# A convolution block in front of an expert stage: tap logits after the convolution in one run, an exponential, transposes and a sum moved

## The reference

```
u  = (x - mean_c(x)) / sqrt(var_c(x) + 1e-6)            # over channels, per pixel
wt = softmax over an axis of length 1 of ((max(u) @ w2.T + b2) - (avg(u) @ w1.T + b1))
x  = x + depthwise_conv3x3(u, wt) + bias + u            # a 3x3 filter per image and channel
t  = tokens of x (32768 rows of 128)
n  = layernorm(t);  gates = n @ Wg + bg;  best two of 8 experts, softmax of their gates
out = t + sum over both of weight * (gelu(n @ W1[e] + b1[e]) @ W2[e] + b2[e])
```

## Time and profile before

| | |
|---|---|
| median of 3 runs | 1534.79 us (1530.91 to 1535.08) |
| the profiled execution | 1534.89 us, its span 1532.4 us |
| PE busy over the span | 1453.9 us (95%) |
| DVE busy | 1308.8 us (85%) |
| ACT busy | 1096.7 us (72%) |
| POOL busy | 961.6 us (63%) |

### The profile page before, as it was taken

One profiled execution on the slowest core, in us unless ns is written; L12 is line 12 of the kernel. 1 busy time (PEld: TensorE's weight loads), 2 busy tenths in 40 slices (PEclk: granted clock), 3 DMA queues, 4 the chain that ended last, 5 costly groups with the idle time before them and its releaser, 6 DMA issues.

```text
span 1532.4 us, 45755 instructions
## 1 busy us (share of the span) xinstructions
PE 1453.9 (95%) x12204; PEld 1114.6 (73%) x12205; DVE 1308.8 (85%) x2676; ACT 1096.7 (72%) x2514; POOL 961.6 (63%) x1069
## 2 busy tenths in 40 slices
PE   5999999999999867999999999999999999999996
PEld 2345454555545433999999999999999999999995
DVE  2468888888888984999999999999989999999995
ACT  5477777878777523777777777777777777777773
POOL 2004455545555674777777777777777777777773
PEclk8899999999999955999999999999999999999998
DMA  4211212121222127111111232223232322222222
GB/s 141 74 38 57 70 63 81 63 75 58 77 69 64 40 71 151 41 47 40 44 43 57 66 93 86 92 86 93 85 94 83 92 86 91 84 86 78 78 75 109
DMA packets 85647, 115.77 MB, mean 76 GB/s; under 512 B 17613, under 2 KB 69865, under 8 KB 85590
## 3 DMA queue, kind: packets, MB, share of 16 engines
q1 hardware_dynamic: 64886, 76.83, 17.0%
q0 software_dynamic: 18112, 34.27, 7.0%
q10 hardware_dynamic: 2592, 4.00, 0.9%
HBM read 60.08 MB, written 58.48 MB: 77 GB/s over the span
## 4 chain that ended last, share of the span: by engine, by line
POOL 38%; PE 24%; issue 23%; DVE 6%; ACT 4%; DMA 2%; POOLq 2%; SPq 1%; ACTq 0%; DVEq 0%
PE psV L902 14%; POOL token_out L542 14%; POOL xn L530 14%; POOL yt L537 9%; PE psA L840 4%; PE psV L849 3%; DVE x L1235 2%; POOL rows_by_pair L512 1%; ACT cv L628 1%; PE psT L884 1%; ACT diag L618 1%; PE psG L886 1%; DMA stage<-in_L_ffn_W_dram 1%; ACT lnv L601 1%; POOLq L542 1%
## 5 line engine op out<-in xcount | busy, mean ns | idle before, releaser
L1495 DVE TENSOR_TENSOR gl<-g,gh 128x512 f16<-128x512 f32 x620 | 489.1, 828 | 71.1 <-ACT gh L777 61.2
L512 POOL DMA_INDIRECT rows_by_pair<-rows,idx x256 | 263.6, 1030 | 318.7 <-issue 196.1
L542 POOL DMA_INDIRECT token_out<-yt,rt x310 | 338.7, 1093 | 184.7 <-POOL yt L537 133.6
L902 PE MATMUL psV<-lp,diag 128*128 128x512 f32 x576 | 274.4, 613 | 20.5 <-ACT cv L628 20.5
L777 ACT ACTIVATE gh<-g 128x512 f16<-128x512 f32 x465 | 274.5, 624 | 16.8
L770 ACT ACTIVATE g<-psT 128x512 f32<-128x512 f32 x310 | 182.2, 597 | 101.3 <-PE psT L1057 74.4
L770 ACT ACTIVATE g<-psV 128x512 f32<-128x512 f32 x310 | 184.8, 597 | 90.1 <-PE psV L1057 62.0
L530 POOL TENSOR_SCALAR xn<-rt 128x128 f32<-128x128 f32 x310 | 221.5, 721 | 14.0 <-DMA rt<-rows_by_pair 10.1
L1078 PE MATMUL psR<-wall,gh 128*128 x1240 | 221.3, 273 | 0.4 <-DVE ya L1512 0.4
L1078 PE MATMUL psG<-wall,gh 128*128 x1240 | 221.3, 273 | 0.0
L902 PEld LDWEIGHTS psV<-lp,diag 128*128 128x128 f32 x576 | 106.2, 193 | 150.9 <-issue 108.2
(11 more groups left out here) (231 smaller groups left out, 2950.2 us busy)
## 6 DMA issues: line engine op xcount, KB each, us to landing
rt<-rows_by_pair SPq DMA_DIRECT2D x155, 133.0 KB, 2.1
xb<-in_x_dram SPq DMA_DIRECT2D x32, 512.0 KB, 3.5
yq<-token_out SPq DMA_DIRECT2D x112, 128.0 KB, 2.4
out_dram<-oq SPq DMA_DIRECT2D x112, 128.0 KB
token_out<-yt,rt POOLq DMA_INDIRECT x310, 2.3
rows_by_pair<-rows,idx POOLq DMA_INDIRECT x256, 2.4
stage<-in_L_ffn_W_dram SPq DMA_DIRECT2D x1, 2048.0 KB, 8.3
ye<-token_out SPq DMA_DIRECT2D x4, 512.0 KB, 4.3
```

The costliest lines, as they stand in the source:

```text
L512: gp.indirect_dma_start(rows_dram, bass.IndirectOffsetOnAxis(ap=idx[p][:, b:b + 1].bitcast(U32), axis=0), rows[p][:, b, :], None).then_inc ...
L542: gp.indirect_dma_start(y_dram, bass.IndirectOffsetOnAxis(ap=rt[r][:, b, ID:ID + 1].bitcast(U32), axis=0), yt[r][:, b, :], None, bounds_ch ...
L902: ins = te.matmul(psConv.rearrange("p (h w) -> p h w", w=WW), diag[k][:, m, :], lp[j][:, y:y + HH // 2, dx:dx + WW], start=(m == 0), stop= ...
L1495: v.tensor_tensor(gl[side][q][:, cols], g[side][:, cols], gh[side][q][:, cols], ALU.subtract).then_inc(lo_done, 1)
```

## The change

Five edits of the order, with the same operations on the same data. On PE all taps of the second image come first, then all 36 tap-logit matmuls, then the centring; and for the first image (k = 0) six blocks of transposes instead of five stand ahead of the variance, the other two are moved between the convolution's halves, and two taps instead of one stand ahead of the second variance. On ACT the tap exponential moves from the end of the step to a place ahead of the second image's last copy, and the first image's `token_std` and `keep` move ahead of its `sum_up`. On DVE the product in `own_places` and the reduction in `number` are only marked, and the sum `den` of the two gate exponentials moves from `weigh` to `number`, ahead of `idx`.

```diff
+    TURN_0 = 6
...
@@ ACT, step
-                    if st_.on(1):
+                    if k == 1 and st_.on(1):
                         sum_up(st_, k)
                     if st_.on(3):
                         token_std(st_, k)
                         keep(st_, k)
+                    if k == 0 and st_.on(1):
+                        sum_up(st_, k)
+                    if k == 1 and st_.on(1):
+                        act.wait_ge(z_ready, st_.count(1, 1, 1))
+                        sc_.activation(ez[:, :, :], zd[:, :, :], ACT.Exp).then_inc(ez_ready, 1)
                     if st_.on(2):
                         take(st_, k, 1)
...
                 if st_.next().on(1):
                     square(st_.next(), 0)
-                if st_.on(1):
-
-                    act.wait_ge(z_ready, st_.count(1, 1, 1))
-                    sc_.activation(ez[:, :, :], zd[:, :, :], ACT.Exp).then_inc(ez_ready, 1)
@@ PE, step (tap_logits loses its quarters and runs all taps)
                     if st_.on(3):
-                        turn(st_, k, 0, TURN_1)
+                        turn(st_, k, 0, TURN_1 if k else TURN_0)
                     if st_.on(1):
                         variance(st_, k, 0)
-                    if st_.on(3):
+                    if k == 1 and st_.on(3):
                         turn(st_, k, TURN_1, NBLK)
...
                     if st_.on(2):
-                        conv(st_, k, 0, 0)
+                        for m in range(2):
+                            conv(st_, k, 0, m)
                     if k == 0 and st_.on(1):
                         variance(st_, k, 1)
...
-                        for m in range(1, len(taps_pe[k])):
+                        for m in range(2, len(taps_pe[k])):
                             conv(st_, k, 0, m)
+                    if k == 0 and st_.on(3):
+                        turn(st_, k, TURN_0, NBLK)
...
-                        for m in range(len(taps_pe[0]) if k == 0 else N_PE - 2):
+                        for m in range(len(taps_pe[k])):
                             conv(st_, k, 1, m)
...
-                for quarter in range(4):
-                    if quarter < 2:
-                        if st_.on(2):
-                            conv(st_, 1, 1, N_PE - 2 + quarter)
-                    elif st_.next().on(1):
-                        centre(st_.next(), 0, quarter - 2)
-                    if st_.on(1):
-                        tap_logits(st_, quarter)
+                if st_.on(1):
+                    tap_logits(st_)
+                if st_.next().on(1):
+                    for h in range(2):
+                        centre(st_.next(), 0, h)
@@ DVE, own_places and number (den leaves weigh)
-                c4.link(v.tensor_tensor(pos[:, :, :], pos[:, :, :], pairs[:, :, :], ALU.mult))
+                c4.mark(v.tensor_tensor(pos[:, :, :], pos[:, :, :], pairs[:, :, :], ALU.mult))
...
-                link(v.tensor_reduce(idf[:, :], pos[:, :, :], AX_X, ALU.add))
+                c4.wait()
+                c4.mark(v.tensor_reduce(idf[:, :], pos[:, :, :], AX_X, ALU.add))
+                dve.wait_ge(e2_ready, st_.count(4, 1, 1))
+                c4.link(v.tensor_tensor(den[:, :], e2[:, :, 0], e2[:, :, 1], ALU.add))
```

More of the change, by code:

```diff
@@ L856, in setup_done, with tap_logits @@
                 pe.wait_ge(s_setup_dve, 2)
[L858 to L865, removed]
+            def tap_logits(st_):
+                pe.wait_ge(pool16_ready, st_.count(1, 1, 1))
+                if st_.on(4):
+                    pe.wait_ge(rank_read, st_.count(4, 1, 1))
+                for tap in range(TAPS):
                     at = R_TAP + 4 * tap
@@ L870, in tap_logits @@
                         last = te.matmul(psR[:, at:at + 2], cwT[:, a, tap, 1, :], both[:, 0:2], start=False, stop=(a == 1), skip_group_check=True)
-                if quarter == 3:
-                    last.then_inc(tap_ready, 1)
+                last.then_inc(tap_ready, 1)
             def turn(st_, k, first=0, end=NBLK):
@@ L1301, in own_places @@
             def own_places(st_):
-                c4.link(v.tensor_tensor(pos[:, :, :], pos[:, :, :], pairs[:, :, :], ALU.mult))
+                c4.mark(v.tensor_tensor(pos[:, :, :], pos[:, :, :], pairs[:, :, :], ALU.mult))
             def number(st_):
-                link = c4.link
-                link(v.tensor_reduce(idf[:, :], pos[:, :, :], AX_X, ALU.add))
+                c4.wait()
+                c4.mark(v.tensor_reduce(idf[:, :], pos[:, :, :], AX_X, ALU.add))
+                dve.wait_ge(e2_ready, st_.count(4, 1, 1))
+                c4.link(v.tensor_tensor(den[:, :], e2[:, :, 0], e2[:, :, 1], ALU.add))
                 if not st_.fixed or (st_.turns(4) > 0 and not st_.last(4)):
@@ L1318, in weigh @@
                 r_ = rows[st_.row_slot(4)]
-                dve.wait_ge(e2_ready, st_.count(4, 1, 1))
-                link(v.tensor_tensor(den[:, :], e2[:, :, 0], e2[:, :, 1], ALU.add))
                 link(v.reciprocal(wa[:, :], den[:, :]))
```

## The result

The changed kernel takes 1511.98 us (median of 4 runs, 1510.42 to 1513.72) against 1533.7 (1530.91 to 1535.08): a ratio of 0.9861, 95% interval 0.9842 to 0.988. The chip's engines go by two names here: PE is TensorE, DVE is VectorE, ACT is ScalarE. The profiled execution took 1510.42 with a span of 1507.6, 24.8 less than the span of before.

A forecast was written before the change was run, and what follows sets the result against it. PE was taken to bound the step, 31.16 us. Gains of 0.12 and 0.85 make 0.97; times 14 is 13.6, less 0.3 plus 0.2 gives 13.5: 1534.9 to 1521.4 us, range 1516 to 1529.

The forecast's parts named there:

- The sum of the step: PE's step of 31.16 us less 0.12 for tap logits and 0.85 for transposes: 30.19, a gain of 0.97.
- I take nothing: ACT's exponential ahead of the last copy: 0 to 0.2 us to spare before PE's variance, counted as no gain or loss.
- the two places named: PE's losses per step: 0.94 us waiting for ACT's copy before the convolution's second half, 0.27 before the second variance.
- the rival on DVE: DVE sets the pace, so its whole 1.39 us wait leaves every step: 19.5 us, total 1515.4; chance 0.07.
- PE's pieces don't fit into 29.8: Argument against DVE setting the pace: PE's work needs about 30.2 us a step, DVE's chain without its wait 29.8.
- the 0.27 that was booked under the two taps: PE's wait before the second variance; two taps instead of one give ACT 0.88 us longer, removing it.
- The exponential's chain: ACT's exponential, copy, then square finished at t = 22.93 us; PE reaches the variance at 22.95, so it just fits.
- The late square: Rival: ACT's square delays PE's variance, each step giving back 0.3 us; gain 9.3, total 1525.6; chance 0.18.
- The slower rival: Exponential stays at t = 22.37 us and blocks ACT's copy and square; 0.4 more per step, total 1540.6; chance 0.07.
- First tokens: ACT's first-image tokens ahead of its sum: costs nothing; PE reaches the second image's transposes no sooner than the centring before.
- DVE's edits: DVE's idle 0.19 and 0.21 us go; 0 in the loop, 0.2 gained on the path to the scatter.
- Start and tail: 12 more tap logits ahead of the second centring half lose 0.3 us; DVE edits add 0.2 at the end.

The follow-up runs named there:

- the load runs: Changed kernel (period 29.77) plus two additions on VectorE each step: 29.77; plus three of the second image's transposes done twice on TensorE: 30.09.
- TURN_0 = 5: Changed kernel with three blocks of transposes behind the convolution instead of two, five ahead of the first variance: period 29.63, 1508.11 us, ratio 0.9845.

## Why the prediction was too small

Three steps of it failed. The sum of the step carried a stretch over as unchanged in which PE was waiting, and priced taps and variances too high. "I take nothing" for the exponential missed that it is a link of the round trip that set the pace. The clock at the start had no term. Of the 8.2 us by which the medians miss the forecast, the step makes 14 x 0.42 = 5.9.

*What bounds the kernel before.* PE does lose time at the two places named. That its own work sets the pace there does not hold: by the two runs with additions on DVE (0.00 and 0.39) it was the round trip over PE, DVE and ACT. In the changed kernel PE does set the pace, at 29.77, so the sentence against the rival on DVE, "PE's pieces don't fit into 29.8", was wrong. The rival's time for a step (1.39) came out and its mechanism did not: two additions on DVE, ahead of its wait, cost nothing in either kernel. That the gain of a step equals DVE's wait is luck. The rule beside it (the Trainium skill, Perfetto Trace Analysis, Identifying the Most-Contended Engine: judge TensorE by MFU and weight loads, not by matmul busy time) would, by the weight loads, have named DVE; the load runs do not agree with it in the changed kernel, +0.33 for TensorE against nothing for VectorE.

*The sum of the step:* 0.97 forecast, 1.39 measured. By stretches of PE's timeline, in one step each:

| stretch | before | forecast | after |
|---|---|---|---|
| convolution to convolution (267.94 / 283.52) | 14.93 | 14.93, unchanged | 14.73 |
| last convolution, logits, centring | 6.42 | 6.30 | 6.25 |
| transposes to the next convolution | 9.81 | 8.96 | 8.79 |

The missing 0.42 is 0.20 + 0.05 + 0.17. The last two are prices: a tap inside a run costs 0.86 (two taps from 307.12 to 308.84, three from 309.70 to 312.27), and the 0.88 had the start of a run behind a wait in it; the variance between the taps costs 0.86 (308.84 to 309.70), not 0.95. The 0.20 is work called unchanged in which PE was in fact waiting. The weight load ahead of the second image's transposes, before and after, and ACT's last operation on the first image's tokens:

```profile
274.06 0.14 PEld L884 LDWEIGHTS psT<-ident,x 128*128 128x128 f32 x1 [0.67 <-issue]
```

```profile
273.75 0.20 ACT L656 ACTIVATE rows<-rstd 128x8 f32<-128x8 f32 x1
```

```profile
289.21 0.14 PEld L883 LDWEIGHTS psT<-ident,x 128*128 128x128 f32 x1 [0.24 <-issue]
```

```profile
287.87 0.20 ACT L657 ACTIVATE rows<-rstd 128x8 f32<-128x8 f32 x1
```

The load is idle 0.43 less, under a name that tells of no wait. But `turn` waits for ACT to have kept the first image's tokens, and in the kernel before the load comes 0.11 to 0.12 behind the end of that operation in each of eight steps; in the changed kernel it comes 1.14 behind it. So it waited for the first tokens; in the run with the transposes alone the profile names this wait (PE psT <- ACT rows). As means of six and seven steps the stretch shrinks by 0.15 (14.92 to 14.76), between the centring and the convolution behind the transposes; in the two steps of the table a shorter wait for ACT's copy, 0.19 against 0.27, adds to it.

*By edits* the split was further off. Logits and exponential were to bring 0.12 and brought 0.72; the transposes were to bring 0.85 and brought 0.67 behind them, nothing without them. The prediction took the exponential only as a possible cost ("I take nothing"); it was the half of the round trip that freed diagonals, logarithm and second variance, and so also the 0.27 that was booked under the two taps: with these two edits and still one tap ahead of it, the second variance starts 0.95 behind that tap, not 1.19.

*The exponential's chain* held: exponential, copy and square in time, no wait before the variance, with 0.45 to spare where it "just fits". The late square came only with a third block moved. *The slower rival* is what the exponential does without the early logits: right in kind, 0.9 a step at full clock, far more with the clock's fall.

*First tokens* cost nothing, as said, and the changed kernel is as fast without that edit. The sentence that PE reaches the second image's transposes no sooner than the centring before them did not hold for the kernel before, as the weight load shows; with the exponential moved alone, first tokens as before, the load is idle 0.25 already.

*DVE's edits* bring nothing in the loop, as said, and the 0.2 at its end was right. From the last row of the pattern to the scatter it is 18.39 in three kernels that have them (the changed one twice, and with the first tokens as before) and 18.64 in the two that don't. By the Trainium skill's rule beside it (VectorE: DVE Perf Modes, The DRAIN you can't avoid) they bring nothing; the trace does not agree there. Whether the 0.25 reaches the end of the span the runs don't show: from the last exponential to there it is 1025.0 and 1024.7 us in the two runs of the changed kernel and 1024.7 without the edits.

*Start and tail.* Forecast 0.3 lost at the start and 0.2 won behind the loop; measured 2.97 + 1.5 won up to the end of the first period and 0.5 to 0.9 behind the loop. The 4.5 go with the clock, which the prediction did not look at: at equal clocks the start is 0.3 sooner, not 0.3 later (last section).

What was to show it: idle of 0.3 to 0.4 ahead of the convolution (0.34), no wait ahead of the softmax, new waits for rstd and ranks (0.22, 0.21), the exponential right behind keep (0.19 idle) were all there; the period and the scatter's start were not.

## What to carry to other kernels

When an engine in a loop looks busy and still waits for others, find the round trip that starts and ends on it, over every engine, before pricing its pieces: an edit on that path is worth little until its slowest link moves, and two edits that bring next to nothing or a loss alone can bring half of the gain together. Add a little work on one engine, ahead of its longest wait and behind it: which of them lengthens the period tells whose time is on the path, better than busy shares do. A stretch called unchanged can still shrink, since a wait can stand in the profile under "issue": see whether the instruction always comes at the same distance behind what its semaphore waits for.

## What the runs showed of the hardware

TensorE's clock at the start is not settled by the order of work alone. Windows of the kernel before, of before with two additions on VectorE ahead of its wait and of before with them inside the softmax (both begin far later), of the changed kernel, and of the one with TURN_0 = 5 (which acts only once there are tokens), columns as above:

```profile
36.00:38.00 2.00, 1.43 (x14) 0.50 0.00 0
44.00:46.00 2.00, 2.00 (x6) 0.83 0.91 326
58.00:60.00 2.00, 2.00 (x3) 0.59 0.02 8
```

```profile
36.00:38.00 2.00, 1.58 (x14) 0.79 0.00 0
42.00:44.00 2.00, 2.00 (x4) 0.58 0.13 40
58.00:60.00 2.00, 2.00 (x6) 1.00 0.01 4
```

```profile
42.00:44.00 2.00, 2.00 (x6) 0.82 0.25 37
58.00:60.00 2.00, 2.00 (x6) 1.00 0.01 4
```

```profile
36.00:38.00 2.00, 1.49 (x3) 0.77 0.00 0
58.00:60.00 2.00, 1.51 (x4) 1.00 0.00 0
```

```profile
42.00:44.00 2.00, 2.00 (x5) 0.82 1.05 399
```

With the same work up to there, the clock goes from 0.50 (1.2 GHz) to 1.00 (2.4 GHz) at 37 us in one execution and at 42 to 45 in another, though PE is busy without a gap from 34 to 36 us in each of these, and in some executions it falls once more. The third exponential starts between 101.0 and 104.1 us in four runs whose start has before's order, and between 95.7 and 98.3 in four with the changed order: 2 to 3 us of a total differ from execution to execution.

What the clock is worth in the profiled pair, runs with equal clocks tell. Where it rises alike, from 42 to 44 us (0.82 in both), the first row of the pattern stands at 47.93 in before's order (additions inside the softmax) and at 47.67 in the changed order (TURN_0 = 5): 0.3 of the 2.97 is left. The first period takes 32.48 in the profile of before, whose clock falls again at 58, and 30.77 in the two kernels with additions, where it doesn't: that is a difference of 1.7, which covers the 1.5. Whether the changed order makes the early rise more likely stays open: the clock rises before 42 us in nine of eleven profiles whose start has the changed order and in one of six with before's, but no run tries why.

In the kernel with the exponential alone the clock fell in the middle of the run, behind a wait of 1.28 us and not in every step; in the kernel before, with waits of 0.85, it stayed at 1.00 there.
